# Constant filler products on TensorE before and inside the attention batches

## The reference

```python
# layer 1: soft alignment of x and y, and its gradient by theta
zx = take(W_embed, x) @ W_proj + b_proj ; zy = likewise of y
theta = einsum('bid,bjd->bij', zx, zy)              # 32 x 128 x 128
aln = vmap(grad(nw_value))(theta, A)                # anti-diagonal recurrence, logsumexp
h = aln
# layer 2: attention on the normalised h, 8 heads of width 16, one number per head for Q and K
A = -(Q[:, :, :, None] - K[:, :, None, :]) ** 2
P = softmax(A / 4) ; O = einsum('bhts,bhse->bhte', P, V)
h = h + O @ Wm + input1
# layer 3: mixture of 8 experts, 2 for each token
h = h + sum_e gate_e * ((silu(x @ W[e]) * (x @ V[e])) @ W2[e])
```

## Time and profile before

| | us |
|---|---|
| median of 3 runs | 864.63 (861.42 to 865.3) |
| the profiled execution, its own time | 863.14 |
| its span, first to last instruction | 860.9 |
| TensorE busy | 487.0 (57%) |
| VectorE busy | 613.6 (71%) |
| ScalarE busy | 365.9 (43%) |
| GpSimd busy | 296.6 (34%) |

### The profile page before, as it was taken

The page is one execution under the profiler, slowest core; times in us unless marked ns, Lnnn a source line. Parts: engine busy times, 40 slices in busy tenths (PEclk is TensorE's granted clock), DMA queues, the critical chain, the costliest instruction groups (busy, mean ns, idle before and its releaser), DMA issues.

```text
span 860.9 us, 13288 instructions
## 1 busy us (share of the span) xinstructions
PE 487.0 (57%) x2622; PEld 423.3 (49%) x2623; DVE 613.6 (71%) x2029; ACT 365.9 (43%) x956; POOL 296.6 (34%) x449
## 2 busy tenths in 40 slices
PE   2200000000013688798899889630699999999960
PEld 1200000000012577697888878630588888888850
DVE  3698989889558876979888765554366666666645
ACT  2244444444213545454454443110365556666630
POOL 1054545445201222221445355337033333333330
PEclk9999999999999999999999999999999999999985
DMA  4599130402343122121211000002111111111109
GB/s 96 103 173 164 28 80 1 80 18 62 75 123 99 49 78 57 54 82 28 69 41 56 10 26 25 26 25 72 30 46 41 43 42 43 41 42 45 43 12 289
DMA packets 113384, 54.17 MB, mean 63 GB/s; under 512 B 56652, under 2 KB 109132, under 8 KB 113251
## 3 DMA queue, kind: packets, MB, share of 16 engines
q1 hardware_dynamic: 106366, 44.60, 22.4%
q0 software_dynamic: 4352, 8.47, 3.0%
q10 hardware_dynamic: 2621, 0.62, 0.5%
HBM read 29.93 MB, written 24.26 MB: 63 GB/s over the span
## 4 chain that ended last, share of the span: by engine, by line
DVE 36%; PE 31%; issue 21%; DMA 5%; SPq 4%; ACT 3%; ACTq 0%; DVEq 0%; POOLq 0%
DVE D L1185 5%; DVE D L1160 5%; PE ps L542 5%; PE ps L748 4%; PE ps L544 4%; PE ps L543 4%; PE ps L728 4%; ACT D L820 2%; DVE D L1151 2%; PE ps L628 2%; DVE rc L1329 2%; PE ps L747 2%; PE ps L633 2%; PE ps L744 2%; DVE ps L1140 1%
## 5 line engine op out<-in xcount | busy, mean ns | idle before, releaser
L633 PEld LDWEIGHTS ps<-va,pt 128*128 128x128 f32 x512 | 137.5, 351 | 0.0
L1035 POOL TENSOR_TENSOR sq<-sq,mn 128x1024 f32<-128x1024 f32 x32 | 67.2, 2099 | 189.9 <-ACT sq L892 185.4
L628 PE MATMUL ps<-eye_sb,sq 128*128 128x128 f32 x256 | 114.7, 454 | 28.8 <-DVE on L1345 28.3
L1071 POOL DMA_INDIRECT y_dram<-on,dest x72 | 70.7, 983 | 164.0 <-DVE on L1488 128.0
L633 PE MATMUL ps<-va,pt 128*128 128x17 f32 x512 | 114.7, 307 | 0.0
L628 PEld LDWEIGHTS ps<-eye_sb,sq 128*128 128x128 f32 x256 | 87.5, 343 | 49.4 <-issue 38.7
L578 PE MATMUL ps<-zdiag,ones_f 32*128 32x32 f32 x2 | 0.6, 406 | 193.1 <-DVE zdiag L1228 193.1
L1020 POOL TENSOR_TENSOR D<-D 128x128 f32<-128x128 f32 x130 | 56.2, 432 | 129.1 <-DVE D L1178 65.1
L578 PEld LDWEIGHTS ps<-zdiag,ones_f 32*128 32x128 f32 x2 | 0.5, 308 | 193.1 <-DVE zdiag L1228 193.1
L1459 DVE TENSOR_TENSOR sq<-sq,ps 128x512 f32<-128x512 f32 x72 | 49.5, 688 | 57.9 <-PE ps L544 42.3
L1044 POOL DMA_INDIRECT xd_dram<-pay,slot x64 | 63.6, 993 | 42.6 <-DVE pay L1408 25.1
(11 more groups left out here) (227 smaller groups left out, 1531.6 us busy)
## 6 DMA issues: line engine op xcount, KB each, us to landing
stage<-xd_dram SPq DMA_DIRECT2D x72, 65.0 KB
D<-th_dram SPq DMA_DIRECT2D x16, 208.0 KB, 4.8
g_dram<-D SPq DMA_DIRECT2D x14, 208.0 KB, 4.6
x_dram<-D SPq DMA_DIRECT2D x14, 208.0 KB, 4.7
h0q<-g_dram SPq DMA_DIRECT2D x8, 256.0 KB, 3.0
gb<-g_dram SPq DMA_DIRECT2D x8, 256.0 KB, 3.4
xf<-x_dram SPq DMA_DIRECT2D x8, 256.0 KB, 3.2
xb<-x_dram SPq DMA_DIRECT2D x8, 256.0 KB, 3.9
```

The source lines that it names most:

```text
L628: last = nc.tensor.transpose(ps[:, 5 + h // 4, T * (h % 4):T * (h % 4) + T], sq[n % 3][:, T * h:T * h + T], eye_sb[:])
L633: m = nc.tensor.matmul(ps[:, 7, (HD + 1) * h:(HD + 1) * (h + 1)], pt[turned % 2][:, T * h:T * h + T], va[q % 2][:, k, h, :], start=True, s ...
L1035: pool.tensor_tensor(v, v, bass.AP(tensor=m.tensor, offset=m.offset, ap=[m.ap[0], [1, NH], [0, T]]), ALU.subtract).then_inc(s_sub, 1)
L1071: pool.indirect_dma_start(y_dram, bass.IndirectOffsetOnAxis(dest[:, c:c + 1], 0), yrow[c], None, bounds_check=2 * NB * T - 1, oob_is_err=F ...
```

## The change

A helper `keep_clock(bank, times)` issues `times` products of 512 columns: weights `below_sb`, the moving operand `wide`, which is `below_sb` read four times over. Their result goes to a PSUM bank whose content nobody reads before the next real product overwrites it. The helper is called at four places: 20 products after alignment step 124, then 85 products after the product of `zdiag`, then in each batch two ahead of the products of `distances` and two at the head of `turn_and_attend`. In the two last places they stand behind the waits that free the bank. That is 105 products before the batches and 32 x 4 = 128 in them. No other engine gets an instruction more or less.

```diff
+            def keep_clock(bank, times):
+                for _ in range(times):
+                    nc.tensor.matmul(ps[:, bank, :], below_sb[:], wide, start=True, stop=True)
+            pe.wait_ge(s_wraw, 1)
+            pe.wait_ge(s_gap, 1)
+            pe.wait_ge(s_lin, STEPS - 6)
+            keep_clock(0, 20)
             pe.wait_ge(s_zd, 1)
-            pe.wait_ge(s_gap, 1)
             nc.tensor.matmul(ps[:, 0, 0:NB], ones_f[64:96, :], zdiag[64:96, :], start=True, stop=True).then_inc(s_zp, 1)
+            keep_clock(1, 85)
...
                 need(pe, s_sq, n)
                 need(pe, s_mn, n)
+                keep_clock(3, 2)
                 for c in range(2):
                     m = nc.tensor.matmul(ps[:, 3 + c, :], qs[q % 2][g, :], kx[q % 2][g, 512 * c:512 * c + 512],
...
                     need(pe, s_pta, pta(n))
                     need(pe, s_ptd, ptd(n))
+                    keep_clock(5, 2)
                 if n > 0:
                     need(pe, s_pta, pta(n))
                     need(pe, s_ptd, ptd(n))
```

More of the change, by code:

```diff
@@ L575, in _ @@
                              start=False, stop=True).then_inc(s_small, 1)
+            b = below_sb[:]
+            wide = bass.AP(tensor=b.tensor, offset=b.offset, ap=[b.ap[0], [0, 4], [1, 128]])
+            def keep_clock(bank, times):
[5 more added lines that the diff above has]
+            keep_clock(0, 20)
             pe.wait_ge(s_zd, 1)
-            pe.wait_ge(s_gap, 1)
             nc.tensor.matmul(ps[:, 0, 0:NB], ones_f[64:96, :], zdiag[64:96, :], start=True, stop=True).then_inc(s_zp, 1)
+            keep_clock(1, 85)
             def turn_tokens(q):
```

## The result

The changed kernel takes 885.31 us (median; 883.63 to 886.85) against 864.26 us of the kernel before (861.42 to 865.3, one more run than above). The ratio is 1.0248, 95% interval 1.0217 to 1.0279: slower by 21 us. The profiled execution took 885.54 us with a span of 883.3, 22.4 us over that of before. An execution more than 1.5% longer than the fastest of its kernel stays out of the ratios given here.

What follows compares the result with a forecast made beforehand. TensorE at 1.2 GHz was taken as the nearer bound, VectorE close behind. Fillers ahead add 0, those in the batches 24 + 4 + 3 = 31 us on 863.1, giving 894 us; range 830 to 912.

Steps and rivals of the forecast that it cites:

- The attention runs at 1.2 GHz: Whole attention before the change: lower clock level despite the column's 1.00; at the higher, TensorE's 7.41 us a batch becomes about 3.7.
- The 20 and the 85: 0 us: Fillers around `zdiag`, ahead of the batches: covered by waits, taken as 0 us; the 85 take 19.6 us at the higher level.
- rival 3: Fillers ahead of the batches never raise the clock: 13.4 us on top of the forecast, 907 us; chance 0.05.
- The speed is lost before the first distances: Between the 85 fillers and the first batch, 252 to 266 us: the clock falls, so the 105 fillers' gain is gone.
- Two and two do not raise the clock: In the batches: four fillers leave the clock at 1.2 GHz; 894 us, own range 880 to 912, chance 0.46.
- The sign named for it: Attention's transposes: still about 450 ns if the forecast is right; a mean under about 400 ns means it is wrong.
- The argument from full weights: Fillers ahead of the batches: their full weights, unlike the preparation's products of 22 and 66 rows, speak against rival 3.
- How much of the 1.70 us a batch is hidden: Batches from 300 to 500 us: 24 add 40.8 us of fillers, 5 to 6 us stay idle, so +24 us.
- The other two terms: Outside 300 to 500 us: fillers add +4 us from 266 to 300 and +3 us from 500 to 560.
- The pair at the transposes is covered by the wait for `normalise`: Second pair of fillers in each batch: 18.4 us of TensorE's idle time, waits for `normalise`, stand behind it.
- Rival 1: In the batches the clock rises and stays up; VectorE's 6.65 us a batch is the bound: 826 us, chance 0.16.
- Rival 2: In the batches the clock repeatedly rises and falls, fast for share s; 846 us at s = 0.3; chance 0.25 over 0.2.

Runs made afterwards that it cites:

- the run with three kinds: Against the kernel before: no fillers in batches; ahead of them 20 bf16 products with 32 weight rows, 45 fp32r products, 45 f32 transposes; one execution, 859.39 us.
- one run of eight: Changed kernel without fillers at the distances, eight at the transposes ahead of the wait for the exponentials: 863.23 us, ratio 0.9987 to the kernel before.
- eight and eight: Changed kernel with eight fillers in place of two at both places of a batch: 869.11 us, ratio 1.0099 to the kernel before.
- four and four: Changed kernel with four fillers in place of two at both places of a batch: 898.44 us against 863.0 for the kernel before.
- six and six: Changed kernel with six fillers in place of two at both places of a batch: 871.62 us, ratio 1.0095 to the kernel before.
- the run with six ahead of the wait: Changed kernel without fillers at the distances, six at the transposes ahead of the wait for the exponentials: 863.14 us, ratio 1.0016 to the kernel before.

## Why the prediction came out as it did

- **The attention runs at 1.2 GHz.** Right, though the clock column said 1.00. The run with fillers only ahead has the same busy times with 0.50 beside them.
- **The 20 and the 85: 0 us.** Right: ratio 1.0011 alone. The 85 took 18.5 us against 19.6 worked out, so rival 3 did not happen.
- **The speed is lost before the first distances.** Right, already in the pause of 4.3 us before the first transposes.
- **Two and two do not raise the clock.** Right but for one stretch of 3.4 us. The sign named for it held: the transposes' mean stayed at 448 ns. The argument from full weights held for the distances (the 32-row run), and the fillers' own kind does raise it where there is enough of it on end. The prediction left open whether the transposes count; the run with three kinds says that they do, with the reservation made there.
- **How much of the 1.70 us a batch is hidden.** The mis-sized term, 300 to 500, put at +24 us and 9.2 to 9.6 us a batch over the whole; measured over the whole 9.00, so this sign of being right did not come. The same 23 batches, from one `distances` to another near the ends of that stretch, before and after:

```profile
303.73:500.56 196.83, 174.49 (x818) 154.14 (x817) 158.84 (x468) 93.23 (x153) 69.59 (x44) 1.00 0.19 53
```

```profile
305.65:519.87 214.22, 211.63 (x909) 165.06 (x908) 161.01 (x471) 93.11 (x154) 70.97 (x45) 0.50 0.16 48
```

They take 17.4 us more. TensorE's busy time grows by 37.1 us, and its idle time falls from 22.3 to 2.6 us, which takes up 19.7. The forecast had 40.8 us of fillers and 16.8 taken up. So 3 of the 6.6 us too many are idle time: 5 to 6 us were left idle in the sum, and only 2.6 stayed. The rest is on the side of the fillers. The prediction counted 24 batches of 8.34 us, but here a batch takes 8.56, so it is 23 (1.7 us). And 23 x 1.70 is 39.1, not 37.1. A likely reason for these last 2 us, not shown: a product is 0.61 to 0.63 us long but the next starts 0.425 us after it, so at each pause a tail counts as busy, and there are fewer pauses now. The other two terms were about right: the first of these `distances` starts 1.9 us later than before (put at 4), and 3.1 us come behind the last (put at 3). 17.4 + 1.9 + 3.1 = 22.4 us, against 31. The own range of the case, 880 to 912, holds the time.
- **The pair at the transposes is covered by the wait for `normalise`.** Not shown: 0.17 us a batch against 0.28 for the pair at the distances is in its direction, but the ratios do not tell the two apart. The idle time takes up most of either pair.
- **Rival 1, up and stays up, 826 us.** No kernel held the speed all the time; the nearest, with 0.76 and 0.78 of it, took 867 and 869 us. Its price is untested at full share, but it let nearly all of VectorE's waits for TensorE go. With one run of eight, at a share of 0.62, they were still 34 us, and with eight and eight, at 0.78, 37.5:

```profile
DVE rc L1343 <- PE ps L621: 16.8, 6, 5.1
DVE pt L1351 <- PE ps L642: 15.0, 7, 2.5
DVE rc L1358 <- PE ps L647: 5.7, 2, 4.4
```

- **Rival 2, (TensorE's work at the lower level + 0.93)/(1 + s).** It did not happen with two and two. With more fillers the formula is near where TensorE is busiest: four and four has 7.41 + 3.40 + 0.93 = 11.74 and s = 0.24, 9.5 us a batch, measured 9.25; eight and eight has 15.14 and s = 0.78, 8.5 us, measured 8.63; six and six, with TensorE idle 22.6 of 200 us, lies off it: 13.44 and s = 0.68, 8.0 us, measured 8.59. With one run of eight it does not: 11.74 and s = 0.62 make 7.2 us, measured 8.33, with TensorE idle for 16% of the time. The step that fails there is that a faster TensorE passes all of its gain on to the batch.

## What to carry to other kernels

Products added only for the clock cost, on an engine that is near its bound, all that its idle time does not take up, here 0.66 of 1.70 us a batch. Few of them were the worst choice: they cost at the lower level and raised the clock too seldom. Before adding any, ask what the next bound is with TensorE at full speed; here it was so close that even a mean clock of 0.8 to 0.9 gave back no more than the fillers took. If they are tried, one run of them ahead of a wait did better here than two behind waits; look in the timeline whether they end before the data that the engine waits for is ready. Do not build up speed ahead of a pause.

## What the runs showed of the hardware

- The clock column of this profile reads 1.00 for all time ahead of the first record. Pairs of one shape in two stages (454 against 274 ns) are the safer reading.
- Not every dense stretch raises the clock: 20 products of 512 columns with 32 weight rows (8.7 us) and 45 fp32r products of 128 columns on full weights (9.9 us) did not; bf16 products of 512 columns on full weights and f32 transposes did.
- The Trainium skill, page "TensorE: Matmul & The Clock Gate", part 4, has transposes not count for the clock. The 45 f32 transposes speeding up from 0.21 to 0.11 us apart do not agree with it, with the reservation above.
- With one run of 8 fillers a batch the clock rose eight times between 430 and 550 us, about every second batch, not in nearly every one as an expectation has it. The time of such a kernel varies by several us from run to run, four and four and the run with six ahead of the wait by 16.
